# Decoder layer on one core: the depthwise convolution of channels 128 to 255 moved from element-wise steps to diagonal matmuls on TensorE

## The reference, cut to what matters

```python
proj = jnp.einsum('btd,ed->bte', x, W_in)            # 256 -> 512
gate, val = (proj[..., :D], proj[..., D:])
g = jax.nn.sigmoid(gate)
v = conv(val, conv_w, padding=2, feature_group_count=D)   # 5 taps along time, each channel by itself
v = v + conv_b
gv = g * v
h = a * h + gv[t]     # a scan along time, a = tanh(a_param)
res = x + y @ W_out.T # then two layer norms
```

## Time and profile before

| what | us |
|---|---|
| median of 3 runs | 835.27 |
| lowest and highest of them | 832.3, 837.21 |
| the profiled execution's own time | 838.04 |
| its span, first to last instruction | 836.2 |
| first block, by the end of its last GpSimd instruction | 203.2 |
| PE busy over the span | 683.0 (82%) |
| DVE busy | 559.9 (67%) |
| ACT busy | 375.9 (45%) |
| POOL busy | 295.2 (35%) |

### The profile page before, as it was taken

The page is one execution under the profiler, slowest core; times in us unless marked ns, Lnnn a source line. Parts: engine busy times, 40 slices in busy tenths (PEclk is TensorE's granted clock), DMA queues, the critical chain, the costliest instruction groups (busy, mean ns, idle before and its releaser), DMA issues. The chain is left out here.

```text
span 836.2 us, 7727 instructions
## 1 busy us (share of the span) xinstructions
PE 683.0 (82%) x2632; PEld 508.1 (61%) x2632; DVE 559.9 (67%) x957; ACT 375.9 (45%) x527; POOL 295.2 (35%) x182
## 2 busy tenths in 40 slices
PE   6885663521676998998998989999679999999996
PEld 2353332411444886786876867878537777777784
DVE  0699767740335489589598697575458777777785
ACT  3616473484343675684774666564331211222101
POOL 0663445633000356356456455233275112221000
PEclk9978895655777999998999999999969999999999
DMA  5102020313100000000000000000161000000001
GB/s 205 50 1 101 0 101 0 101 50 120 57 0 0 1 1 0 1 1 0 1 1 0 1 0 2 1 1 0 29 223 50 26 1 26 25 26 26 26 1 51
DMA packets 18119, 27.33 MB, mean 33 GB/s; under 512 B 1312, under 2 KB 11168, under 8 KB 18080
## 3 DMA queue, kind: packets, MB, share of 16 engines
q1 hardware_dynamic: 18080, 26.84, 9.3%
HBM read 18.44 MB, written 8.39 MB: 32 GB/s over the span
## 5 line engine op out<-in xcount | busy, mean ns | idle before, releaser
L703 PE MATMUL psum<-slots_hi,w_hh 128*128 128x512 f32 x576 | 184.6, 403 | 12.3 <-DVE gru L967 12.3
L1248 PE MATMUL psum<-w_expert,slots_hi 128*128 128x512 f32 x512 | 165.7, 405 | 0.0
L884 POOL TENSOR_TENSOR gru<-slots_full,gru 128x512 f32<-128x512 f32 x48 | 74.7, 1557 | 221.9 <-ACT gru L799 221.9
L703 PEld LDWEIGHTS psum<-slots_hi,w_hh 128*128 128x128 f32 x576 | 110.6, 193 | 39.4 <-DVE gru L967 14.5
L1322 DVE SCALAR_TENSOR_TENSOR y_group<-psum,sel,y_group 128x256 f32<-128x256 f32 x224 | 108.3, 484 | 33.6 <-PE psum L1248 13.9
L703 PE MATMUL psum<-slots_lo,w_hh 128*128 128x512 f32 x288 | 115.1, 400 | 0.0
L1248 PEld LDWEIGHTS psum<-w_expert,slots_hi 128*128 128x128 f32 x512 | 96.2, 189 | 25.7 <-issue 1.9
L1248 PE MATMUL psum<-w_expert,slots_lo 128*128 128x512 f32 x256 | 101.5, 397 | 0.0
L703 PE MATMUL psum<-at,v_ih 128*128 128x512 f32 x288 | 90.8, 396 | 3.3 <-DVE at L960 3.3
L349 PE MATMUL psum<-x_fm,w_in 128*128 128x512 f32 x128 | 63.1, 655 | 19.7 <-ACT g L206 12.3
L967 DVE SCALAR_TENSOR_TENSOR gru<-psum,vec,gru 128x512 f32<-128x512 f32 x48 | 36.0, 749 | 60.3 <-PE psum L703 54.8
(11 more groups left out here) (162 smaller groups left out, 1134.5 us busy)
## 6 DMA issues: line engine op xcount, KB each, us to landing
x_fm<-in_xT SPq DMA_DIRECT2D x4, 1024.0 KB, 6.5
x_tm<-in_x SPq DMA_DIRECT2D x4, 1024.0 KB, 6.8
x_scratch<-slots_full SPq DMA_DIRECT2D x8, 512.0 KB, 3.0
gru<-x_scratch SPq DMA_DIRECT2D x8, 512.0 KB, 6.5
out<-out_group SPq DMA_DIRECT2D x8, 512.0 KB, 3.0
w_expert_raw<-in_expertT SPq DMA_DIRECT2D x4, 512.0 KB, 6.7
whh_raw<-in_whhT SPq DMA_DIRECT2D x1, 768.0 KB, 4.8
wih_raw<-in_wihT SPq DMA_DIRECT2D x1, 768.0 KB, 6.9
```

Of the source, the lines that this page charges most:

```text
L703: last = pe.matmul(psum[:, bank, :], w, d, start=start and i == 0, stop=stop and i == len(pairs) - 1)
L884: pool.tensor_tensor(DF(u), full[:, c, seq(k, h), blk(j)], X(u), ALU.subtract).then_inc(d_pool, 1)
L1248: last = pe.matmul(psum[:, EB + p, :], slots[d][:, c, b, cols], ew[w][:, c, piece(p)], start=m == 0, stop=m == len(todo) - 1)
```

## The change

For the half c = 1 the five taps are no longer computed on ScalarE, GpSimd and VectorE. VectorE sets up five 128x128 matrices once, each with one tap's 128 weights on its diagonal (`diag`); `convolve(b)` on TensorE then multiplies them with the shifted rows of `val`, five float32 matmuls of 128x512 into each of the two banks TB that the transposes use, ten for a batch; and VectorE adds the bias and multiplies with the gate in one step for each bank (`taps(b, 1)`), from PSUM into `cvs`. ScalarE's two tap passes and GpSimd's `last_tap` and `apply_gate` for c = 1 go. `tap` shrinks to the half that is left. The half c = 0 stays as it was. TensorE's queue gets `convolve(0)` after `project(1)`, `convolve(1)` after `output(0)`, and `convolve(b + 2)` as the last step of the loop's round b.

```diff
--- before.py
+++ after.py
@@ -115,7 +115,8 @@
         xt_in = sem("xt_in")
         gate_mm, val_mm, gate_ev, val_ev = sem("gate_mm"), sem("val_mm"), sem("gate_ev"), sem("val_ev")
         tap_act, tap_pool, conv = sem("tap_act"), sem("tap_pool"), sem("conv")
-        gated, scanned = sem("gated"), sem("scanned")
+        gated, gated_tail, scanned = sem("gated"), sem("gated_tail"), sem("scanned")
+        diag_set, conv_mm = sem("diag_set"), sem("conv_mm")
         out_mm, res_done, xb_done = sem("out_mm"), sem("res_done"), sem("xb_done")
         bn1, agg1, bn2, agg2, mul_done, add_done = (
             sem("bn1"), sem("agg1"), sem("bn2"), sem("agg2"), sem("mul_done"), sem("add_done"))
@@ -130,7 +131,8 @@
         g = sb1("g", [P, 2, C, T])
         val = sb1("val", [P, C, T + 2 * HALO])
         cvs = [sb1("cv", [P, C, T])[:], full[:, :, B - 1, :]]
-        tap = full[:, :, B - 2, :]
+        tap = full[:, 0, B - 2, :]
+        diag = full[:, 1, B - 2, 0:K * P].rearrange("p (k n) -> p k n", k=K)
         wi = sb1("w_in", [P, C, 2 * D])
         wo = sb1("w_out", [P, C, D])
         lw = sb1("ln_w", [P, D])
@@ -205,20 +207,24 @@
                         act.wait_ge(gate_mm, J * n + j + 1)
                         act.activation(g[:, b % 2, c, cols_of(j)], psum[:, GB + j, :],
                                        ACT.Sigmoid).then_inc(gate_ev, 1)
-                    if b > 0:
-                        act.wait_ge(conv, TAPS * (n - C + 1))
+                    if b > 0 and c == 0:
+                        act.wait_ge(conv, TAPS * b)
+                    if b > 0 and c == 1:
+                        act.wait_ge(conv_mm, J * b)
                     for j in range(J):
                         act.wait_ge(val_mm, J * n + j + 1)
                         act.activation(val[:, c, HALO + j * BANK:HALO + (j + 1) * BANK],
                                        psum[:, VB + j, :], ACT.Copy).then_inc(val_ev, 1)
+                    if c == 1:
+                        return
                     act.wait_ge(val_ev, J * n + J)
                     if b > 1:
                         act.wait_ge(scanned, n - 2 * C + 1)
                     act.activation(cvs[b % 2][:, c, :], val[:, c, 0:T], ACT.Identity, bias=col(c, V_CB),
                                    scale=col(c, 0)).then_inc(tap_act, 1)
                     if b > 0:
-                        act.wait_ge(tap_pool, n - C + 1)
-                    act.activation(tap[:, c, :], val[:, c, K - 1:K - 1 + T], ACT.Copy,
+                        act.wait_ge(tap_pool, b)
+                    act.activation(tap, val[:, c, K - 1:K - 1 + T], ACT.Copy,
                                    scale=col(c, K - 1)).then_inc(tap_act, 1)
 
                 def window(b):
@@ -280,13 +286,12 @@
             @block.gpsimd
             def _(pool):
                 def last_tap(b, c):
-                    n = C * b + c
-                    pool.wait_ge(tap_act, 2 * n + 2)
-                    pool.tensor_tensor(cvs[b % 2][:, c, :], cvs[b % 2][:, c, :], tap[:, c, :],
+                    pool.wait_ge(tap_act, 2 * b + 2)
+                    pool.tensor_tensor(cvs[b % 2][:, c, :], cvs[b % 2][:, c, :], tap,
                                        ALU.add).then_inc(tap_pool, 1)
 
                 def apply_gate(b, c):
-                    pool.wait_ge(conv, TAPS * (C * b + c + 1))
+                    pool.wait_ge(conv, TAPS * (b + 1))
                     pool.tensor_tensor(cvs[b % 2][:, c, :], cvs[b % 2][:, c, :], g[:, b % 2, c, :],
                                        ALU.mult).then_inc(gated, 1)
 
@@ -317,20 +322,14 @@
                 pool.memset(epsc[:, 2:3], EPS_LN).then_inc(consts_set, 1)
                 pool.wait_ge(consts_in, 96)
                 last_tap(0, 0)
-                last_tap(0, 1)
                 apply_gate(0, 0)
-                apply_gate(0, 1)
                 last_tap(1, 0)
-                last_tap(1, 1)
                 for b in range(B):
                     if b + 1 < B:
                         apply_gate(b + 1, 0)
                     add_bias(b)
-                    if b + 1 < B:
-                        apply_gate(b + 1, 1)
                     if b + 2 < B:
                         last_tap(b + 2, 0)
-                        last_tap(b + 2, 1)
                     if b > 0:
                         new_slots(b - 1)
                 new_slots(B - 1)
@@ -368,38 +367,70 @@
                         pe.wait_ge(n2_done, NT * b + t + 1)
                         if t % 2 == 0 and H2 * b + q > 1:
                             pe.wait_ge(x1_ev, H2 * b + q - 1)
+                        if t % 2 == 0 and q < 2:
+                            pe.wait_ge(gated_tail, J * min(b + 3, B))
                         for c in range(C):
                             at = (t % 2) * D + c * P
                             last = pe.transpose(psum[:, TB + q % 2, at:at + P],
                                                 res[:, b % 2, t, c * P:(c + 1) * P], ident[:])
                         last.then_inc(x1_T, 1)
 
+                def convolve(b):
+                    n = C * b + 1
+                    pe.wait_ge(val_ev, J * n + J)
+                    if b > 0:
+                        pe.wait_ge(gated_tail, J * b)
+                    if b > 2:
+                        pe.wait_ge(x1_ev, H2 * (b - 2))
+                    for j in range(J):
+                        for k in range(K):
+                            last = pe.matmul(psum[:, TB + j, :], diag[:, k, :],
+                                             val[:, 1, k + j * BANK:k + (j + 1) * BANK], start=k == 0, stop=k == K - 1)
+                        last.then_inc(conv_mm, 1)
+
                 pe.wait_ge(w1_in, 16)
                 project(0)
+                pe.wait_ge(diag_set, K)
                 project(1)
+                convolve(0)
                 pe.wait_ge(consts_in, 96)
                 for b in range(B):
                     output(b)
+                    if b == 0:
+                        convolve(1)
                     if b + 2 < B:
                         project(b + 2)
                     if b > 0:
                         transposes(b - 1)
+                    if b + 2 < B:
+                        convolve(b + 2)
                 transposes(B - 1)
 
             @block.vector
             def _(dve):
                 def taps(b, c):
-                    n = C * b + c
-                    dve.wait_ge(tap_pool, n + 1)
+                    if c == 1:
+                        for j in range(J):
+                            dve.wait_ge(conv_mm, J * b + j + 1)
+                            dve.wait_ge(gate_ev, J * (C * b + 1) + j + 1)
+                            if b > 1:
+                                dve.wait_ge(scanned, C * (b - 1))
+                            dve.scalar_tensor_tensor(out=cvs[b % 2][:, c, cols_of(j)], in0=psum[:, TB + j, :],
+                                                     scalar=col(c, V_CB), in1=g[:, b % 2, c, cols_of(j)], op0=ALU.add,
+                                                     op1=ALU.mult).then_inc(gated_tail, 1)
+                        return
+                    dve.wait_ge(tap_pool, b + 1)
                     for i, k in enumerate(range(1, K - 1)):
                         if i:
-                            dve.wait_ge(conv, TAPS * n + i)
+                            dve.wait_ge(conv, TAPS * b + i)
                         dve.scalar_tensor_tensor(out=cvs[b % 2][:, c, :], in0=val[:, c, k:k + T], scalar=col(c, k),
                                                  in1=cvs[b % 2][:, c, :], op0=ALU.mult, op1=ALU.add).then_inc(conv, 1)
 
                 def scan(b, c):
-                    n = C * b + c
-                    dve.wait_ge(gated, n + 1)
+                    if c == 0:
+                        dve.wait_ge(gated, b + 1)
+                    else:
+                        dve.wait_ge(gated_tail, J * (b + 1))
                     dve.tensor_tensor_scan(out=g[:, b % 2, c, :], data0=acol[:, c:c + 1].broadcast_to([P, T]),
                                            data1=cvs[b % 2][:, c, :], initial=0.0, op0=ALU.mult,
                                            op1=ALU.add).then_inc(scanned, 1)
@@ -447,6 +478,8 @@
                     dve.memset(ones_h[mine, other].bitcast(F32), 0.0).then_inc(consts_set, 1)
                 dve.wait_ge(consts_in, 96)
                 dve.wait_ge(consts_set, 14)
+                for k in range(K):
+                    dve.tensor_scalar(diag[:, k, :], ident[:], col(1, k), None, ALU.mult).then_inc(diag_set, 1)
                 taps(0, 0)
                 taps(0, 1)
                 scan(0, 0)
```

## The result

The changed kernel takes 837.75 us (median of 17 runs, 835.92 to 841.82); the kernel before, measured beside it, 834.92 us (17 runs, 829.98 to 838.43). The ratio is 1.004 with a 95% interval of 1.002 to 1.0059: 2.8 us slower. The interval leaves out 1, so the loss is clear of the measurement's noise; it is smaller than the 0.5% that the prediction called "no change", though the interval's upper end, 0.59%, is not. The forecast was 837.2 in a range of 832 to 843.

The account below looks back on a forecast made before the run. VectorE's written order set the pace at 60 to 120 us; now TensorE's queue would, convolutions ahead of awaited work. Plus 2.4 us at offsets(2), less 0.5, gave plus 1.9: 839.9 profiled, 837.2 against the median; range 832 to 843.

Parts of the forecast that it names:

- 1: output(0) starts: Start: convolve(0) follows project(1), and batch 0's scans wait behind its second tail; output(0) 7.2 us later, from 44.50.
- 2: offsets(0): After output(0): VectorE waits about 6 us for convolve(1), with offsets(0) queued behind the tail; plus 8.9, from 61.39.
- 3: output(1) starts: project(2) and then convolve(2) stand ahead of output(1) in TensorE's queue; it starts 14.7 us later, from 78.14.
- 4: offsets(1): Way back begins: output(1) at full clock and 4.8 us of taps gone; offsets(1) only 7.4 us later, from 96.72.
- 5: output(2) starts: ScalarE's last read of batch 0 at 122.7, then convolve(3) ahead of output(2); plus 13.9, from 117.32.
- 6: residual(2) starts: The load of x, which held residual(2) until 126.05 before, now lands under the convolution; residual(2) starts at 133.2.
- 6: offsets(2): output(2) at full clock, and 4.76 us of taps become 1.5 hidden; offsets(2) only 2.4 us later, from 140.04.
- Step 7: After offsets(2): no convolution left and no taps were there, so the same chain moves as a whole.
- the correction in the last step: Same rules put the kernel before at offsets(2) 0.5 us later than its trace; taken off, leaving plus 1.9.
- Rival A: convolve(2) and convolve(3) start at a slow clock behind gaps: 840.7 us; all convolutions at half clock: 854.4; chance 0.22.
- Rival B: Start costs less: warm clock at output(0), 835.2 us; over 4.2 faster needs cheap convolutions (2.2 us each: 818); chance 0.06.
- Rival C: Batch 2's load of x, not TensorE, stays the last wait at residual(2): 834 us, output(2) before 128; chance 0.05.

Follow-up runs that it names:

- e5: Changed kernel with convolve(0) put between the two halves of project(1) in TensorE's queue: 829.3 us against 834.8 for the kernel before.
- e2: Changed kernel with each convolution's matmuls computed twice, output unchanged: 873.6 us, 36 more than the changed kernel.
- e4: Kernel before, with the loads of x for batches 2 and 3 issued ahead of the stores of batches 0 and 1: 830.3 us against 834.2.
- e3: Changed kernel with the loads of x for batches 2 and 3 issued ahead of the stores of batches 0 and 1: 837.1 us.
- e1: Changed kernel with only the middle tap of five computed, 2 matmuls a batch instead of 10: 822.1 us against 834.2 for the kernel before.
- e6: Changed kernel with convolve(b+1) right behind output(b) for every b: 844.2 us against 834.8 for the kernel before.
- e7: Changed kernel with VectorE's bias and gate step moved from ahead of the offsets to between the two scans: 843.9 us against 834.8 before.
- e8: Changed kernel with the edits of e3, e5 and e7, and convolve(b+1) behind output(b) inside project(b+2): 823.9 us against 834.8 for the kernel before.
- e9: e8 with the loads of x for batches 2 and 3 put back behind the stores: 831.0 us against 834.7 for the kernel before.

## Why the prediction was right, point by point

| step | forecast, us | trace after, us |
|---|---|---|
| 1: output(0) starts | 51.75 | 51.87 |
| 2: offsets(0) | 70.3 | 70.94 |
| 3: output(1) starts | 92.8 | 93.64 |
| 4: offsets(1) | 104.1 | 104.81 |
| 5: output(2) starts | 131.2 | 131.79 |
| 6: residual(2) starts | 133.2 | 133.81 |
| 6: offsets(2) | 142.4 | 142.95 |

- The terms: a convolution took 8.75 us from its first record to the end of its last (8.6 forecast, 8.6 apart in the queue); a tail step 0.75 us alone and 1.38 for two in a row. The projection's records were the right price for a matmul with diagonal weights.
- The tails don't take turns with GpSimd. The last two ran from 140.97 to 142.35, the first of them wholly inside a GpSimd pass, with no stretch at all (and so did the first of the two at 102.82, inside the pass from 101.52 to 103.87):

```profile
139.67 2.35 POOL L302 TENSOR_TENSOR x_tm<-x_tm,ln_b 128x1024 f32<-128x1024 f32 x1 [1.09 <-DVE res L444]
```

  By the rule of the Trainium skill ("SBUF — State Buffer", section SBUF: two separate sides) that was cited for it, this is what should be seen, and the trace agrees: 0.69 us each.
- The set-up of the diagonals took 1.07 us at 10.94, under VectorE's wait for the first batch: nothing, as forecast.
- Steps 1 to 3 (the loss) are borne out by experiments: e5 takes back step 1 and keeps the gain to the end, and in e2 all that is added to the convolutions arrives at the end. Steps 4 to 6 (the way back) are read from the trace: output(2) is 14.5 us late and offsets(2) 2.9. Their largest part, that the late load of x had held up residual(2) in any case, has e4 beside it; what the taps and the full clock gave back was not measured apart.
- Step 7, that the rest moves as a whole, holds: plus 2.9 at offsets(2), plus 2.9 at output(3) (158.11; forecast 157), plus 3.1 at the block's end (206.3; forecast 205).
- The term that was off is the correction in the last step. The walk gave plus 2.4; I took off 0.5 because the same rules reach offsets(2) of the kernel before too late. The trace shows plus 2.9 there, so every step of the walk after was a little early (0.1 to 0.8 us), not late, and in this pair of traces the correction had the wrong sign. That leaves 1.9 forecast against 2.8 measured, which the measured interval (1.7 to 4.9 us) does not tell apart.
- That the steps agree within 0.8 us is in part luck: e3's trace, of the changed kernel but for a load that nothing waited for, has output(2) 1.5 us earlier. The traces before and after happen to start alike (projections of 30.41 and 30.27 us, where e3 took 29.40).
- Two sums in the prediction are a little off, without effect on its result: step 5's terms (104.1 and 21.4 less 3.0) make 122.5, not 122.7; and a gain of over 4.2 us would need 6.1 of the convolutions' 34.4 us to go, so matmuls under about 82% of their rows, not 85%.
- Rival A (slow clock) did not happen: ahead of convolve(2) and convolve(3) TensorE paused 0.69 and 0.78 us only, and their 20 records took 8.85 and 8.83 us. The condition it was tied to, a longer pause, did not come about.
- Rival B: output(0) began at 1.2 GHz behind 5.32 us of idle (granted clock 0.50 from 51.87 to 56.00; 9.78 us for its 32 records, where output(1) took 7.07). Its price for a cheap convolution was 17 us below before; e1, at 1.88 us a convolution, came out at 12 below, so that price was too high by 5. The spacing rule of the Trainium skill ("TensorE: Matmul & The Clock Gate", section Back-to-back issue gap) is a quarter of what a float32 matmul takes here: 20 records in 8.75 us are 10 matmuls, 0.86 us each against 0.216.
- Rival C: output(2) started at 131.8, not before 128, and e3 shows the load without effect.

## What to carry to other kernels

Work that is moved to an engine with time to spare is still put somewhere in that engine's queue: walk the queue, and ask for every step behind the new one who waits for it. Here 34 us of new matmuls gave plus 3 us in one order, plus 9 in two others (e6, e7), minus 5.5 in a fourth (e5) and minus 11 in a fifth (e8, with 4 us that the early loads also give the kernel before), with the same instructions. After each new order look at what it leaves bare: in e6, e7 and e9 VectorE ended up waiting 5.7 to 10.5 us at a residual for the load of x. An edit that does nothing now, as the early load in e3, can be worth several microseconds once the wait ahead of it is gone, so trying such edits one at a time can miss it.

## What the runs showed of the hardware that was not expected

- A convolution's 20 records behind short pauses (0.69 and 0.78 us) and output(0) in e5, with no pause, all ran at 2.4 GHz, where output(0) behind 5.32 us of idle began at 1.2; keeping TensorE busy at the start gave output(0) back 2.7 us (9.78 to 7.07) beside what the order gave.
- GpSimd's passes against three taps of VectorE cost VectorE 5.1 us and GpSimd 1.9 us over their times alone (8.96 against 3.9 and 6.60 against 4.7, in e4).
- What follows the first block, by the same instructions, took 629.3 to 632.9 us from the next block's first VectorE instruction to the end of the span, in the traces of all eleven kernels. A single trace's span tells changes of 3 us only if the block itself is looked at.
